# Routed rows' scatters cut into pieces between the attend products of the last attention

## The reference, cut to what matters

```python
def _L3_xattn_ref(q, k, v, mask, Wq, bq, ...):          # 16 heads of 8 features
    scores = jnp.einsum('bhqd,bhkd->bhqk', query, key) / np.sqrt(D_K)
    attn = jax.nn.softmax(jnp.where(mask == 0, -1e9, scores), axis=-1)
    x = jnp.einsum('bhqk,bhkd->bhqd', attn, value)      # the "attend" products
    return x.transpose(...).reshape(B, S, D_MODEL) @ Wo.T + bo
def _L3_ffn_ref(x, gate_w, gate_b, w1, b1, w2, b2):
    topv, topi = lax.top_k(flat @ gate_w + gate_b, 2)   # the routing
    ...                                                 # out += gelu(x W1e + b1e) W2e * weight, 8 experts
x = x + tanh(g_xattn[3]) * _L3_xattn_ref(_layernorm(x), ctx_1024, ctx_1024, ...)
x = x + tanh(g_ffn[3]) * _L3_ffn_ref(_layernorm(x), ...)
```

## Time and profile before

| what | value |
|---|---|
| runs, us | 1941.26, 1941.89, 1953.97 |
| profiled execution: time and span, us | 1947.2 |
| PE busy, PEld, DVE, ACT, POOL | 83%, 62%, 64%, 62%, 38% |
| mean granted clock of TensorE | 0.908 |
| last attention in the trace, us | about 1405 to 1746 |
| scatters L1044 | 64, of 957 to 1348 ns, from 1516.5 to 1768.0 us |

### The profile page before, as it was taken

The page is one execution under the profiler, slowest core; times in us unless marked ns, Lnnn a source line. Parts: engine busy times, 40 slices in busy tenths (PEclk is TensorE's granted clock), DMA queues, the critical chain, the costliest instruction groups (busy, mean ns, idle before and its releaser), DMA issues. The chain is left out here.

```text
span 1947.2 us, 38941 instructions
## 1 busy us (share of the span) xinstructions
PE 1623.4 (83%) x12739; PEld 1206.7 (62%) x12739; DVE 1241.5 (64%) x3348; ACT 1208.4 (62%) x4192; POOL 742.3 (38%) x712
## 2 busy tenths in 40 slices
PE   4399999699999769999689956999579887865994
PEld 3355554389999546666489855545446655644994
DVE  5499998488888756767467756213357656554444
ACT  2189998189999457888567743433158666641444
POOL 2145555245555531111057835002222343333452
PEclk9799999599999879999899977999679999877997
DMA  3320000110000142423191022100043442313224
GB/s 126 82 97 1 1 1 1 40 38 2 2 1 2 42 95 62 114 73 89 23 320 62 1 87 82 46 0 1 14 115 102 111 122 86 88 46 104 70 72 156
DMA packets 63558, 125.36 MB, mean 64 GB/s; under 512 B 10894, under 2 KB 27457, under 8 KB 61241
## 3 DMA queue, kind: packets, MB, share of 16 engines
q1 hardware_dynamic: 53658, 103.10, 19.0%
q10 hardware_dynamic: 5328, 11.01, 1.8%
q0 software_dynamic: 4384, 8.89, 1.3%
HBM read 89.43 MB, written 49.39 MB: 71 GB/s over the span
## 5 line engine op out<-in xcount | busy, mean ns | idle before, releaser
L1548 ACT ACTIVATE L_E<-L_sc,L_negm 128x128 f32<-128x128 f32 x1024 | 299.9, 403 | 161.3 <-DVE L_negm L1407 160.7
L593 ACT ACTIVATE B_E<-B_logits,B_m 128x32 f32<-128x32 f32 (+1 forms) x1792 | 364.3, 374 | 9.2 <-DVE B_m L562 8.1
L599 POOL TENSOR_TENSOR B_E<-B_E,B_r 128x512 f32<-128x512 f32 x256 | 268.0, 1047 | 263.8 <-DVE B_r L581 263.8
L1407 DVE TENSOR_REDUCE L_negm<-L_sc 128x4 f32<-128x512 f32 x256 | 174.8, 685 | 92.3 <-PE L_sc L1659 81.2
L562 DVE TENSOR_REDUCE B_m<-B_logits 128x16 f32<-128x512 f32 (+1 forms) x256 | 172.6, 675 | 37.9 <-PE B_logits L553 30.7
L1657 PE MATMUL L_sc<-KS,L_QS 128*128 128x512 f32 x256 | 145.8, 570 | 55.6 <-DMA L_QS<-L_qlo 20.4
L576 DVE TENSOR_REDUCE B_r<-B_E 128x16 f32<-128x512 f32 (+1 forms) x256 | 172.7, 675 | 2.5 <-POOL B_E L599 1.3
L1556 ACT ACTIVATE L_PT<-L_pt 128x512 f32<-128x512 f32 x256 | 166.4, 652 | 6.2 <-DMA picked_rows<-A_ys 5.9
L1667 PE MATMUL L_pt<-ident,L_E 128*128 128x128 f32 x1024 | 160.8, 281 | 0.8 <-ACT L_PT L1556 0.8
L551 PE MATMUL B_logits<-B_phihi,B_xhi 128*128 128x512 f32 x256 | 153.2, 599 | 5.3 <-DVE B_philo L538 2.5
L1667 PEld LDWEIGHTS L_pt<-ident,L_E 128*128 128x128 f32 x1024 | 127.6, 146 | 24.3 <-issue 3.1
(11 more groups left out here) (348 smaller groups left out, 3559.9 us busy)
## 6 DMA issues: line engine op xcount, KB each, us to landing
route_rows<-in_F_fill SPq DMA_DIRECT2D x33, 516.0 KB, 19.9
KS<-L_ksplit SPq DMA_DIRECT2D x180, 64.0 KB
L_QS<-L_qsplit SPq DMA_DIRECT2D x42, 256.0 KB
F_xg<-route_rows SPq DMA_DIRECT2D x71, 64.5 KB
ew<-in_expert_w SPq DMA_DIRECT2D x1, 4096.0 KB
L_cT<-in_ctxT SPq DMA_DIRECT2D x16, 256.0 KB
F_w<-in_F_w SPq DMA_DIRECT2D x2, 2048.0 KB
F_yl<-F_y_rows SPq DMA_DIRECT2D x16, 256.0 KB, 5.8
```

The source lines that it names most:

```text
L593: ins = nc.scalar.activation(e[:, cols], self.bank(k)[:, cols], ACT.Exp, bias=self.m[:, k % 4, g:g + 1])
L599: self.st.nc.gpsimd.tensor_tensor(e, e, self.r[:, k % 2, :].unsqueeze(2) .to_broadcast([128, self.ng, self.size]), ALU.mult).then_inc(self ...
L1407: nc.vector.tensor_reduce(negm[:, k % 4, :], sc[k % 2][:].rearrange("p (h k) -> p h k", h=NHG), AX.X, ALU.max, negate=True).then_inc(s["ma ...
L1548: ins = nc.scalar.activation(e[:, h * 128:(h + 1) * 128], sc[k % 2][:, h * 128:(h + 1) * 128], ACT.Exp, bias=negm[:, k % 4, h:h + 1])
```

## The change

It takes the two calls of `route.scatter` out of the POOL program of the last attention and puts in five places at which two, three, two and one scatters are issued (and, for the last of these groups, the six that are left). Ahead of each piece POOL waits until a given run of attends is finished.

```diff
+            def scatter_between(m, n, w, puts):
+                if not (route and 0 <= m < NG - 2):
+                    return
+                g.wait_ge(s["av_done"], min(n * UG + w - ATTEND + 1, NU))
+                route.scatter(g, m, puts)
...
             for n in range(NG):
+                scatter_between(n - 3, n, 1, range(2, 5))
                 if n + 1 < NG:
                     split("k", n + 1)
+                scatter_between(n - 3, n, 3, range(5, 7))
                 if route and n >= 2:
                     route.complete(g, n - 2)
                 if route:
                     fold(n)
                 if n + 1 < NG:
                     split("q", n + 1)
-                if route and n >= 2:
-                    route.scatter(g, n - 2, range(2))
+                scatter_between(n - 3, n, 9, range(7, 8))
                 if n:
                     tail.gpsimd(g, n - 1, (n - 1) % 2)
-                if route and n >= 2:
-                    route.scatter(g, n - 2, range(2, route.PUTS))
+                scatter_between(n - 2, n, UG - 1, range(2))
             if route:
+                scatter_between(NG - 3, NG, UG, range(2, route.PUTS))
                 route.complete(g, NG - 2)
             tail.gpsimd(g, NG - 1, (NG - 1) % 2)
```

## The result

Against 1945.04 us before (median of four runs, 1941.26 to 1953.97) the changed kernel took 1896.35 us (median of four, 1891.12 to 1900.81): a ratio of 0.9752, 95% interval 0.9721 to 0.9783. Repeated later, it took 1895.87 us at a ratio of 0.9760 (0.9729 to 0.9791). The prediction was 1911 us with a range from 1899 to 1934.

What follows compares the result with a forecast made beforehand. The prediction took POOL's scatters slowing PE's attends as the bound. Removing 48.4 us and putting in 17.9 gave a 30.5 us gain: 1916.7 from the profiled 1947.2, 1911 as the median of runs, range 1899 to 1934.

Steps and rivals of the forecast that it cites:

- What bounds: Last attention: POOL's eight scatters a group slow PE's attends to about a sixth of their speed; key and query transfers do not.
- Removed, w = 1 to 3: Five groups' stretches from w = 1 to w = 3 fall to 4.69 us each, saving 38.2 us.
- Removed, w = 13 to 15: Six groups with scatters each save 0.71 us from w = 13 to w = 15, 4.3 us together.
- Removed at the end: The attention stage's last two runs would finish at 1727.4 instead of 1733.31, saving 5.9 us.
- Put in: Pieces overlapping the next runs of attends cost up to 3.3 us a group, 17.9 us in all.
- The signs: Expected profile: w = 3 to w = 5 takes 5 to 6 us, a group 34 to 36 us.
- The lower bound: Pieces' overlap with attends, counting nothing after the last issue: 5 x 1.2 + 0.5 put in, 41.9 us gain, 1900 us.
- Waits: POOL's waits ahead of pieces stay hidden: key split in time, query split with 0.8 us to spare.
- The end of the stage: Six scatters before the last L208 stay hidden behind DVE's routing by 0.8 us or more; otherwise up to 2 us.
- pieces that reach 2.5 us: Pieces slow attends until 2.5 us after their last issue: gain 13.4 us, time 1928 us; chance 0.20.
- The slower case: Same longer reach, with three stretched runs a group each costing 1.5 times their stretch: 1946 us; chance 0.10.
- Nothing changes: The place in the group, not POOL, stretches the runs of attends: 1942 us; chance 0.10.

Runs made afterwards that it cites:

- e3: Changed kernel with the scatters of the attention and the waits for them left out; median 1903.87 us, ratio to before 0.9733 to 0.9815.
- e1: Changed kernel without its waits for finished runs, scatters at the same places in POOL's program; median 1947.30 us, ratio to before 0.9997 to 1.0052.
- e12: Changed kernel with one wait a group, for the run of w = 15, and all eight scatters behind it; median 1937.99 us.
- e16: Changed kernel without scatters in the attention, POOL held until the run of w = 5 is finished before complete and fold; median 1905.38 us.
- e2: Changed kernel with pieces of four and four, behind the runs of w = 15 and w = 1; median 1919.09 us, ratio to before 0.9822 to 0.9871.
- e6: Kernel before, each indirect scatter of the attention writing 16 of the 129 elements of every row into its own table; median 1945.70 us.
- e9: Kernel before, each indirect scatter of the attention writing only 32 of its 128 rows; median 1949.34 us, ratio to before 1.0028 to 1.0074.
- e4: Kernel before, the attention's 48 indirect scatters turned into plain POOL transfers of the same rows to fixed rows; median 1900.57 us.
- e11: Changed kernel with pieces of three, three, one and one in place of two, three, two and one; median 1911.18 us.
- e7: Kernel before, the last attention's attend products with 128x128 weights in place of 128x32; median 2039.89 us, ratio to before 1.0466 to 1.0578.
- e13: Changed kernel with pieces of three, three and two behind w = 15, 1 and 3, none at w = 9; median 1905.30 us.

## Where the prediction was right, and where it failed

**What bounds: right.** The scatters, not the transfers of keys and queries, held the runs of w = 15 and w = 1. e3 takes them out, e1 and e12 put the block back. That the attends themselves run at a sixth of their speed, as the prediction read it, is not shown: what is measured is that their completion comes late.

**Removed, w = 1 to 3 (38.2 us): right.** It measured 61.60 - 23.03 = 38.6 us.

**Removed, w = 13 to 15 (4.3 us): wrong.** Nothing is removed there: 4.74 us in the changed kernel and in e3. The 4.04 us of the earlier trace rows belong to group 1, which has no rows to rank and place yet; DVE does 11 operations in 2.52 us there and 12 in 3.10 us in the group with scatters. "Without scatters" was also "without routing", and I read the one as the other. The hole of 1.00 us behind the run of w = 13 was real, but w = 15 did not wait for it.

**Removed at the end (5.9 us): about right.** From the start of the last run to the last attend it was 1732.61 - 1725.44 = 7.2 us and is 1683.34 - 1681.66 = 1.7: 5.5 us. The lag of the last attends is still there, 0.57 us.

**Put in (17.9 us): the step that failed.** Its places were right and its size was not. By e16 the pieces cost 0.7 to 2.8 us in all. Two things are in it. The hold itself was taken at 3.3 us a group, and the lags show 1.5 us: nothing in w = 1, 0.5 in w = 3, 1.0 in w = 5. The 1.2 us of reach behind the last issue was not far off (0.6 to 1.0 us measured), but I charged it in full to the run of w = 1 as well, though by my own numbers that run starts 1.0 us after the piece ahead of it is issued (T + 4.64 against T + 3.6). And I charged a held completion as lost time. PE's next products do not wait for `av_done`; the waiter that counts is DVE's inversion, it idled 0.66 us, and nothing behind it moved. The excess of 7.6 us in the earlier trace rows came from lags of up to 6 us, and dividing it down to a lag of 1 us assumed a straight line that is not there: 1.36 us are nearly free, 2 to 3.5 us cost 4.5 us a group (e2). The signs said the same: w = 3 to w = 5 takes 3.87 us and not 5 to 6, and a group 33.2 us and not 34 to 36. The lower bound, "nothing" for the tail of a piece, still charged 5/6 of the overlap of issue times, 6.5 us in all, and with the 4.3 us of the step before on the other side the range ended at 1899.

**The sum.** With 38.6 + 5.5 removed and 0.7 to 2.8 put in, the gain is 41 to 43 us; the two traces have 43.3 and 45.3 in S. Two stretches that the sum does not have are seen in the first: w = 5 to w = 7 is 1.6 us shorter over the five groups (17.0 against 18.6), w = 7 to w = 9 2.4 us longer (21.1 against 18.7). The errors of 4.3 and of about 16 us were of opposite sign; that the forecast missed the range by under 3 us owes something to this.

**Waits: right. The end of the stage: a small miss.** The key and query splits are ready in time, and no group starts late. From the last inversion to DVE's first operation of the next stage it was 13.4 us and is 14.4, in both traces, though DVE's routing begins its last operation 0.4 us sooner (11.3 in place of 11.8). The prediction had the six scatters hidden behind that routing. But in both kernels POOL's first instruction of the next stage comes 4.95 us after the end of L208, and the scatters move L208 by 1.0 us.

**The rivals.** Of pieces that reach 2.5 us there is no sign: the run of w = 3 is released 1.0 us after its last scatter's issue. The slower case needed three stretched runs a group; e2, with two, shows something of its form, at 22.7 us, with four scatters a piece. "Nothing changes", with the Trainium skill's rule (SBUF — State Buffer, "Who interferes with whom") that a DMA never contends with a compute engine, is refuted as a forecast by e1 against the changed kernel: the same indirect transfers with and without the waits are about 50 us apart. What holds PE is not shown to be the data moved, since the hold does not go with the bytes (e6, e9); e4 agrees with the rule for plain transfers.

## What to carry to other kernels

Spread POOL's indirect transfers with waits, not with program order alone: without waits POOL ran ahead here and closed the gaps (e1). Before a held completion is charged, ask who waits for it and how much slack that engine has; a cost measured with the slack used up cannot be scaled down in proportion. A stretch that serves as "without" must lack only the one thing in question: here group 1 lacked the routing too. And a move on one engine moves all that stands behind it in its queue: e11 lost 7.4 us not by its scatters but by the arithmetic that came earlier.

## What had not been expected of the hardware

An indirect transfer on POOL holds the completion of PE's attends, though their recorded starts stay on time: lags of 6 to 7.5 us beside eight in a row, with 128 rows of 516 bytes, 128 of 64 bytes and 32 of 516 bytes alike. A plain transfer of the same rows on POOL leaves 0.32 us. With pieces of up to four, in groups 3 to 6, the first attend of a held run is counted 0.55 to 0.98 us after the end of the last issue of its piece, in all seven traces that have such pieces.

The hold begins with an attend and takes what is queued behind it. In the changed kernel, scores and transposes that PE starts beside the piece of w = 1, ahead of the run of w = 3, are counted after 0.40 and 0.29 us (1588.01 to 1588.41, 1588.56 to 1588.85), as elsewhere. In the kernel before, six products of PE that start behind the held run, from 1603.46 to 1606.13, are counted in their order within 0.25 us, from 1609.95 to 1610.19. And two held attends are counted 0.15 us apart in the changed kernel (1591.28 and 1591.43), undisturbed ones 0.44. So it may be less the multiplying that is slow than its end that is told late; inside the block of eight, though, the two attends of w = 15 are counted 3.66 us apart (1604.86 and 1608.52), and which of the two it is stays open. The last stage's products beside scatters are not held (0.29 us from start to count throughout), and the 128-column attends of e7 are; why these two differ stays open.

A DVE operation of 0.19 us between SBUF tensors lasted until POOL's arithmetic beside it ended (1.35 and 2.13 us). POOL's work coming 0.9 us sooner cost 7.4 us over the stage (e11 against e13), more than all the pieces of the changed kernel.
